# A Perceiver layer on one core: new order of the vector and matrix work in the last batch of attention, and a later wait for the last attention store

## The reference, cut to what matters

```python
x = x + xattn(layernorm(x), ctx_1024, ...)   # cross attention, 8 batches of 128 queries, 16 heads of 32
x = x + mamba(layernorm(x), ...)             # the "mixer": projection, convolution, scan, output
x = x + moe_ffn(layernorm(x), ...)           # convolution, 8 experts, feed-forward

# xattn: x is (8, 128, 512), ctx_1024 is (8, 2048, 512)
scores = einsum('bhqd,bhkd->bhqk', Q, K) / sqrt(32)
attn = einsum('bhqk,bhkd->bhqd', softmax(scores), V)
out = attn.reshape(8, 128, 512) @ Wo.T + bo
# mamba begins with: xr = layernorm(x) @ w_in + b_in ; w_in is (512, 2048)
```

## Time and profile before

| | |
|---|---|
| Runs | 2110.43 us median of 3 (2106.59 to 2114.09) |
| The profiled execution | 2113.07 us, its span 2111.2 us |
| Busy share of the span | PE 94%, DVE 68%, POOL 56%, ACT 42% |
| Last batch of attention | from about 1097 to 1240 us of the span |
| Start of `mixer_in` | 1240.03 us |

### The profile page before, as it was taken

One profiled execution on the slowest core, in us unless ns is written; L12 is line 12 of the kernel. 1 busy time (PEld: TensorE's weight loads), 2 busy tenths in 40 slices (PEclk: granted clock), 3 DMA queues, 4 the chain that ended last, 5 costly groups with the idle time before them and its releaser, 6 DMA issues. The chain is left out here.

```text
span 2111.2 us, 41942 instructions
## 1 busy us (share of the span) xinstructions
PE 1991.5 (94%) x15559; PEld 1420.4 (67%) x15559; DVE 1437.0 (68%) x1472; ACT 884.8 (42%) x1267; POOL 1177.6 (56%) x843
## 2 busy tenths in 40 slices
PE   6989999999999999999998879899999999899999
PEld 3767777777777777777764458555555554378874
DVE  5126766666666666666667737399999994846655
ACT  1124444444444444444434544466676651133310
POOL 3126666666666666666657621189989992322200
PEclk9999999999999999999998889999999999999999
DMA  4545465555555555555553220310040003012101
GB/s 175 153 141 168 152 179 162 173 171 163 175 156 174 161 171 169 167 169 164 166 168 106 76 62 1 81 42 1 1 120 1 1 25 101 0 46 70 55 0 41
DMA packets 180470, 227.38 MB, mean 108 GB/s; under 512 B 21456, under 2 KB 111824, under 8 KB 174128
## 3 DMA queue, kind: packets, MB, share of 16 engines
q1 hardware_dynamic: 180272, 224.68, 34.9%
HBM read 151.07 MB, written 73.53 MB: 106 GB/s over the span
## 5 line engine op out<-in xcount | busy, mean ns | idle before, releaser
L452 POOL TENSOR_TENSOR a_half<-a_pt 128x1024 f32<-128x1024 f32 x128 | 306.9, 2397 | 348.9 <-ACT a_pt L519 339.3
L519 ACT ACTIVATE a_pt<-a_shift 128x2048 f32<-128x2048 f32 x128 | 245.2, 1916 | 482.3 <-PE a_o L834 371.8
L633 DVE TENSOR_TENSOR a_shift<-a_s,a_neg_rows 128x2048 f32<-128x2048 f32 x113 | 259.0, 2292 | 170.2 <-ACT a_neg_rows L536 170.2
L620 DVE TENSOR_REDUCE a_top<-a_s 128x128 f32<-128x2048 f32 x113 | 258.7, 2290 | 47.4 <-PE a_s L787 47.3
L746 PE MATMUL a_pj<-l_x_hi,l_w_hi 128*128 128x512 f32 x448 | 198.7, 443 | 0.0
L1221 POOL TENSOR_TENSOR s_even_drive<-s_du,l_rows 128x512 f32<-128x512 f32 x128 | 162.7, 1272 | 63.1 <-DMA s_c_row<-bc_scratch 60.4
L443 POOL TENSOR_TENSOR l_x_lo<-a_raw,l_x_hi 128x512 fp32r<-128x512 f32 x120 | 152.9, 1274 | 73.8 <-ACT l_x_hi L506 73.8
L746 PE MATMUL a_pj<-l_w_hi,l_x_hi 128*128 128x512 f32 x448 | 185.5, 414 | 0.0
L1229 POOL TENSOR_TENSOR s_odd_seen<-s_odd_state,s_c_row 128x512 f32<-128x512 f32 x128 | 162.3, 1268 | 34.0 <-DVE s_odd_state L1360 14.5
L1421 PEld LDWEIGHTS s_ps<-s_diag,s_du_t 128*128 128x128 f32 x1024 | 135.9, 194 | 61.9 <-issue 61.9
L748 PE MATMUL a_pj<-l_x_lo,l_w_hi 128*128 128x512 f32 x448 | 177.4, 396 | 0.0
(11 more groups left out here) (235 smaller groups left out, 3981.1 us busy)
## 6 DMA issues: line engine op xcount, KB each, us to landing
kv_scratch<-a_k_new SPq DMA_DIRECT2D x128, 256.0 KB, 2.5
kv_scratch<-a_v_new SPq DMA_DIRECT2D x128, 256.0 KB, 3.7
a_stack<-kv_scratch SPq DMA_DIRECT2D x512, 64.0 KB, 2.3
a_v<-kv_scratch SPq DMA_DIRECT2D x32, 1024.0 KB, 6.2
a_raw<-in_ctx SPq DMA_DIRECT2D x120, 256.0 KB, 3.4
a_q_stack<-q_scratch SPq DMA_DIRECT2D x128, 64.0 KB, 2.1
s_c_row<-bc_scratch SPq DMA_DIRECT2D x32, 256.0 KB, 5.9
e_ew_raw<-in_ew SPq DMA_DIRECT2D x8, 1024.0 KB, 4.8
```

The costliest lines, as they stand in the source:

```text
L452: nc.gpsimd.tensor_tensor(half[:], w[:, 0:2], w[:, 2:4], ALU.add).then_inc(halved, 1)
L519: nc.scalar.activation(pt_head(g, p), shift[:].rearrange("p (i n) -> p i n", n=BANK), ACT.Exp).then_inc(exped, 1)
L620: dve.tensor_reduce(top[:], s_ps[:].rearrange("p i n -> p (i n)").rearrange("p (k q) -> p q k", q=L), AX.X, ALU.max).then_inc(blocked, 1)
L633: dve.tensor_tensor(shift[:].rearrange("p (k q) -> p k q", q=L), s_ps[:].rearrange("p i n -> p (i n)").rearrange("p (k q) -> p k q", q=L), ...
```

## The change

Four edits in `attention` and `mixer_in`:

1. `scale_and_shift` (seven times) and its copy in `mixer_in` make the shift factor with a `tensor_scalar` of two scalars (one from memory, one constant) in place of a `scalar_tensor_tensor` with a second tensor input.
2. `statistics` (`bn_stats`) is issued on DVE after both `shift_half`, no longer before them.
3. PE issues `project_output` step 0 (of the odd head before) or step 3 (of the even head before) between the two half scores of the next head, no longer ahead of both.
4. `a_stored` becomes a semaphore of the layer. SP no longer waits for the last store at the end of `attention`; in `mixer_in` it first issues the seven small loads, then waits for the store, then loads `at` and the two quarters of `w_in`.

```diff
@@ class Mixing / attention: semaphore a_stored is now ln.a_stored
@@ attention, SP
             store_out(B - 1, GROUPS - 1)
-            sp.wait_ge(a_stored, 16 * GROUPS * B)
@@ attention, DVE, scale_and_shift
-                dve.scalar_tensor_tensor(out=shift_by[:, j:j + 1], in0=mv[:, j, 0:1], scalar=-1.0, in1=rstd[:, j:j + 1],
-                                         op0=ALU.mult, op1=ALU.mult).then_inc(ln.scaled, 1)
+                dve.tensor_scalar(shift_by[:, j:j + 1], mv[:, j, 0:1], rstd[:, j:j + 1], -1.0, ALU.mult, ALU.mult)\
+                   .then_inc(ln.scaled, 1)
@@ attention, DVE, mixer_rows and the loop over heads
                 if batch_at(h, 3) is not None:
                     add_output(batch_at(h, 3))
-                    statistics(batch_at(h, 3))
...
                 for s in range(2):
                     shift_half(h, s)
+                if batch_at(h, 3) is not None:
+                    statistics(batch_at(h, 3))
@@ attention, PE, last batch
             for h in range(1, H):
-                for s in range(2):
-                    half_scores(h, s)
+                half_scores(h, 0)
+                project_output(h - 1, 1, (0,))
+                project_output(h - 1, 2, (3,))
+                half_scores(h, 1)
                 turn_half(h, 0)
...
                 weigh_last(B - 1, h // HG, h % HG, False)
-                project_output(h, 1, (0,))
-                project_output(h, 2, (3,))
@@ mixer_in, SP
+            for dst, src in ((bi, b_in), (wc, w_conv), (bc, b_conv), (wx, w_x)) + to_load:
+                sp.dma_start(dst[:], src).then_inc(w_in_s, 16)
+            sp.wait_ge(ln.a_stored, 16 * KC * B)
             sp.dma_start(at[:], a_scratch[J]).then_inc(a_in, 16)
             for s in range(2):
                 sp.dma_start(wi_raw[:, s], mix.w_in[:, :, mix.quarter(2 + s)]).then_inc(wi_in[s], 16)
-            for dst, src in ((bi, b_in), (wc, w_conv), (bc, b_conv), (wx, w_x)) + to_load:
-                sp.dma_start(dst[:], src).then_inc(w_in_s, 16)
@@ mixer_in, DVE
-            dve.scalar_tensor_tensor(out=shift_by[:], in0=mv[:, 0:1], scalar=-1.0, in1=rstd[:], op0=ALU.mult,
-                                     op1=ALU.mult).then_inc(ln.scaled, 1)
+            dve.tensor_scalar(shift_by[:], mv[:, 0:1], rstd[:], -1.0, ALU.mult, ALU.mult).then_inc(ln.scaled, 1)
```

More of the change, by code:

```diff
@@ L61 @@
     SIGNALS = ("o_made", "added", "chain", "var_ready", "root_ready", "scaled", "normed", "turned", "hi_out", "lo_out",
-               "biased", "wi_hi_out", "wi_lo_out")
+               "biased", "wi_hi_out", "wi_lo_out", "a_stored")
     ORDER = (2, 0, 1, 3)
@@ L83 @@
     wi_lo_out: object
+    a_stored: object
     def quarter(self, n):
@@ L273, in attention @@
         (small_in, chi_out, clo_out, projected, k_out, v_out, ones_out, scored, blocked, top_turned, negated, widened,
-         neg_turned, rows_out, shifted, exped, halved, quartered, parted, weighed, totaled, inv_out, out_ready, a_stored) = st.sems(
+         neg_turned, rows_out, shifted, exped, halved, quartered, parted, weighed, totaled, inv_out, out_ready) = st.sems(
             "small_in", "chi_out", "clo_out", "projected", "k_out", "v_out", "ones_out", "scored", "blocked",
             "top_turned", "negated", "widened", "neg_turned", "rows_out", "shifted", "exped", "halved", "quartered",
-            "parted", "weighed", "totaled", "inv_out", "out_ready", "a_stored")
+            "parted", "weighed", "totaled", "inv_out", "out_ready")
         raw_in = st.sems(*[f"raw_in{k}" for k in range(KC)])
@@ L384, in store_out @@
                 sp.wait_ge(out_ready, GROUPS * b + g + 1)
-                sp.dma_start(a_scratch[b, :, g, :], out_t[:, g % 2, :]).then_inc(a_stored, 16)
+                sp.dma_start(a_scratch[b, :, g, :], out_t[:, g % 2, :]).then_inc(ln.a_stored, 16)
             def heads(b, first, projects, final):
@@ L412, in load_outputs @@
                     sp.wait_ge(ln.o_made, j - 1)
-                sp.wait_ge(a_stored, 16 * GROUPS * (j + 1))
+                sp.wait_ge(ln.a_stored, 16 * GROUPS * (j + 1))
                 sp.dma_start(at[:, j % 2], a_scratch[j]).then_inc(at_in[j % 2], 16)
@@ L660, in finish_group @@
                 if stored:
-                    dve.wait_ge(a_stored, 16 * (GROUPS * b + g - 1))
+                    dve.wait_ge(ln.a_stored, 16 * (GROUPS * b + g - 1))
                 dve.tensor_tensor(out_t[:, g % 2, :], o_ps[:, :L], inv_t[:], ALU.mult).then_inc(out_ready, 1)
```

## The result

| | before | changed |
|---|---|---|
| Median of the runs | 2110.43 us | 2118.84 us (2116.19 to 2123.99, 9 runs) |
| Ratio | | 1.0040, 95% interval 1.0030 to 1.0051 |
| Profiled execution, span | 2113.07, 2111.2 us | 2118.75, 2116.9 us |
| L646 of head 1 to L646 of head 15 | 120.98 us | 131.31 us |
| Start of `mixer_in` | 1240.03 us | 1247.15 us |

The forecast was 2107.9 us with a range to 2115.0. The kernel is 8.4 us slower, outside the range and on the other side. The last batch of attention alone is 10.3 us longer. In the two profiled executions the stretch from L646 of head 15 to the mixer's first product then gave 2.4 us back (16.6 for 19.0), and the rest of the kernel 1.4 (869.7 for 871.1).

The account below looks back on a forecast made before the run. A chain through all engines was taken to set the pace in the last attention batch, neither PE nor DVE being full. Heads -3.3 and mixer +0.8 make -2.5 us, from 2110.43 to 2107.9; range 2101.5 to 2115.0.

Parts of the forecast that it names:

- The sum for the heads: Last attention batch, head 4 to head 15: 91.65 us now, 88.1 after at full clock, that is -3.5.
- -1.8 (lower-clock stretches as now) and -6.5 (none left): Bounds on the last attention batch's gain in us, by whether PE's lower-clock stretches stay or vanish; value taken -3.3.
- 4 to 4.5 us of the 91.65: Heads 4 to 15 before the change: the part of their time put down to PE at its lower clock.
- makes a new wait before half 0 in every even head: Last attention batch: edit 3's new PE wait, named as the argument against the rival of a restored clock (-5.7 us, 2104.7).
- Outside these heads: Last attention batch: head 15 gains about 1.2 us into the tail, head 1 gains 1.0, head 3 0 to 0.6.
- the rival on POOL: Odd heads: the new shift factor still waits for POOL, shift 0.9 us late, 3.4 of the gain lost: 2111.3; chance 0.08.
- Half 1 pays more: Last batch: L900 before the late half costs 2.05 us, not 1.06, in several heads; heads gain 0: 2111.2; chance 0.12.
- value +0.8: Mixer's first stage: loss in us from the later load of `at`, PE standing still 2.9 before L1111; bounds 0 to +4.4.
- The rival on PE's clock in the mixer: Mixer's first stage: the wait for `at` puts PE at half rate, up to 11.8 us more: 2119.7; chance 0.04.

Follow-up runs that it names:

- e1: Kernel before with only the two-scalar shift factor and the statistics behind the shifts: 2102.67 us, ratio 0.9969 to the kernel before.
- e5: Changed kernel plus throw-away filler products in PE's holes of the last batch: 2103.15 us, ratio 0.9957 to the kernel before.
- e3: Kernel before with only the last store awaited in the mixer and the small loads first: 2111.67 us, ratio 1.0003 to the kernel before.
- e8: Changed kernel with only step 0 between the score halves, step 3 back ahead of both: 2114.41 us, ratio 1.0017 to the kernel before.
- e9: Changed kernel with the product behind both score halves and filler products in PE's holes of the last batch: 2099.19 us, ratio 0.9931 to the kernel before.
- e6: Changed kernel without products between the score halves, plus filler products in PE's remaining holes: 2103.05 us, ratio 0.9955 to the kernel before.
- e13: e10 with the outputs loaded first in the mixer, then the small loads, then the quarters: 2093.14 us, ratio 0.9917 to the kernel before.
- e4: Changed kernel without the products between the score halves, its other three edits kept: 2101.80 us, ratio 0.9965 to the kernel before.
- e10: e9 with filler products in the tail of attention too: 2095.17 us, ratio 0.9924 to the kernel before.

## Why the prediction was wrong, step by step

- **Edit 1** was right: 0.21 us for the forecast 0.15, in all seven places. The Trainium skill (SBUF — State Buffer, "SBUF: two separate sides") speaks of a lock for two SBUF inputs and for two-port modes; its first half agrees with the stall that went. The 0.21 us beside a running L452 show no lock for the new form; whether a form of one element enters such a mode at all, no run here tells.
- **Edit 2** was right: shift 1.57 to 1.73 us after L646 in odd heads, in the mean of heads 5 to 15 1.24 earlier than before, for the forecast 1.25. With edit 1 it gains 7.9 us (e1). I priced the odd heads' gain right but credited it to a kernel in which edit 3 takes it away.
- **Edit 3** is the step that failed: "The sum for the heads", with its bounds of "-1.8 (lower-clock stretches as now) and -6.5 (none left)". Head 4 to head 15 took 1230.59 - 1128.51 = 102.1 us, not 88 to 92. The geometry was right: 88.1 us was the sum at full clock, and e5, which stays there, takes 88.4 (7.95 us per plain head for 7.87). Wrong was the term for the lower clock, "4 to 4.5 us of the 91.65", and with it the upper bound. I let the stretches at 1.2 GHz stay as they were or vanish; they grew, to 102.1 - 88.4 = 13.7 us in these heads and 18.5 in the whole batch. I had written that edit 3 "makes a new wait before half 0 in every even head", and counted it only against the gain. I also never set it against edits 1 and 2 alone, which would have shown 7.24 for 7.87 in each even head (7.22 and 7.95 measured).
- **Outside these heads**: the tail gained 2.4 us for the forecast 1.2, but heads 1 to 3 gained 0.1 (29.2 us for 29.3) where I had counted 1.0 to 1.6. The bounds do not follow exactly from their terms, which give -1.2 and -6.4 for -1.8 and -6.5, and in the rival on POOL the shift of odd heads would stay 0.56 late at the mean stall, as its sum has it, not 0.9; neither bears on the miss.
- The rival **"Half 1 pays more"** named the place and the 2.05 us at the lower clock, but priced it to come out at 0. It was the true case, with the batch at +10.3.
- **Edit 4**: value +0.8, measured -0.1 us in the stage; alone (e3) +0.4 there (21.18 for 20.74), and 1.0003 (0.9991 to 1.0015) in the total. The terms were off and cancelled: the seven small issues took 3.5 us and not 4.65, and the first tile ran wholly at 1.2 GHz (5.5 us for 4.4), so PE waited 1.30 and not 2.9. No idle PE before the turn, and ACT's first tile 6.6 us earlier in the stage (1254.05 - 1247.19 = 6.9 for 13.5): right. The rival on PE's clock in the mixer did not come in the changed kernel: L1112 took 3.70 us for 3.60. It did in e8, e5 and e9: 5.20, 5.40 and 6.48 us for the same product, behind waits for the outputs of 2.52, 2.76 and 3.37.

What stays open: why a low stretch lasts some 13 us in heads 1, 5, 9 and 13 of the changed kernel and 3 to 4 in head 5 of the kernel before, behind waits of about the same length. Head 3 of the changed kernel has the same waits of 1.07 and 0.95 us as head 5, and there the low stretch lasts some 3 us.

## What to carry to other kernels

A product that fills a wait costs little; the same product between two halves that the next engine is waiting for cost 0.73 us of its 1.06 here, once per round, at full clock, and more where the clock fell. Where the granted clock is under 1.00, no order of work may be costed at one clock: bound it with the low stretches longer as well as gone, and count each new wait of PE as a possible cause of them. Behind both halves was the right place for the product here, and throw-away products in the holes are a quick test of whether the clock is what is lost.

## What the runs showed of the hardware that was not expected

- Adding 128x128 products made the kernel 15.7 us faster, with nothing else changed (e5): PE's granted clock went from 0.70 and 0.79 to 1.00. The Trainium skill (TensorE: Matmul & The Clock Gate, "What's actually happening") says that the throttled clock is the default and activity releases it; e5 agrees.
- A stage some 500 us further on took longer in some executions with fillers: from its first to its last product the experts took 352.7 us in e5 and e6 and 353.2 in e13, 349.8 to 349.9 in the kernel before, the changed one and e4. The granted clock is lower there: 0.77 in e5 from 1812 to 1862 us, 0.84 in the same stretch of the kernel before (1822 to 1872). Why is open, since e9 and e10 with fillers did not show it and e8 without any took 1.2 us longer too.
- The same seven small loads were issued in 3.5 us ahead of the two 1 MB loads and in 4.65 us behind them, and landed 1.6 to 3.8 us after issue, not 6.8 to 7.6.
